# The router of a mixture-of-experts block as four f32r passes with its weights stationary, its results moved by 32x32 transposes on VectorE and small transfers

## What is computed

```python
x = x + attn(layernorm(x))         # linear attention: Q, K, V by 64; energy = K^T V per sequence
x = x + ffn(layernorm(x))
# ffn, on h = layernorm(x):
scores = sigmoid(h @ Wr)                       # 8 experts
_, idx = top_k(scores + router_bias, 2)
w = take_along_axis(scores, idx); w = w / (sum(w) + 1e-9)
cw = zeros(T, 8).at[rows, idx].add(w)
hid = silu(h @ Wg[e]) * (h @ Wu[e])            # experts 0 to 3, 128 wide
routed = sum_e cw[:, e] * (hid @ Wd[e])
routed += cw[:, 4] * h + cw[:, 6] * h + cw[:, 7] * relu(h)
out = routed + causal_depthwise_conv(h, 4 taps)
```

## Time and profile before

| | us |
|---|---|
| median of 3 executions | 893.69 (892.45 to 894.4) |
| the execution profiled | 893.6 |
| its span in the profile | 891.8 |
| PE busy | 855.9 |
| DVE busy | 741.1 |
| ACT busy | 628.7 |
| POOL busy | 572.7 |

### The profile page before, as it was taken

One profiled execution on the slowest core, in us unless ns is written; L12 is line 12 of the kernel. 1 busy time (PEld: TensorE's weight loads), 2 busy tenths in 40 slices (PEclk: granted clock), 3 DMA queues, 4 the chain that ended last, 5 costly groups with the idle time before them and its releaser, 6 DMA issues.

```text
span 891.8 us, 16729 instructions
## 1 busy us (share of the span) xinstructions
PE 855.9 (96%) x5437; PEld 754.3 (85%) x5437; DVE 741.1 (83%) x2056; ACT 628.7 (71%) x1238; POOL 572.7 (64%) x654
## 2 busy tenths in 40 slices
PE   5789999999999999999999999999999999999997
PEld 4668989898888888988889888888888898788876
DVE  5758889988888998888898888899888887767775
ACT  5676777777687777778677777777777775655643
POOL 3336776667676657667666767666576766556663
PEclk9989999999999999999999999999999999999999
DMA  9111434543334543343544343454424344433333
GB/s 286 57 52 47 137 121 142 143 117 99 95 119 142 144 142 68 114 129 120 143 143 114 101 115 99 143 144 142 119 72 119 101 114 119 111 104 100 106 91 84
DMA packets 79446, 103.86 MB, mean 116 GB/s; under 512 B 6528, under 2 KB 58880, under 8 KB 79360
## 3 DMA queue, kind: packets, MB, share of 16 engines
q1 hardware_dynamic: 74752, 86.02, 30.4%
q0 software_dynamic: 4608, 16.78, 10.0%
HBM read 68.96 MB, written 17.04 MB: 96 GB/s over the span
## 4 chain that ended last, share of the span: by engine, by line
PE 66%; DVE 13%; POOL 12%; issue 5%; ACT 4%; DMA 0%; POOLq 0%; ACTq 0%; DVEq 0%
PE ps_gu L406 9%; PE ps_gu L408 9%; PE ps_gu L407 9%; POOL enx L1368 7%; PE ps_y L406 5%; PE ps_y L408 5%; PE ps_y L407 5%; PE ps_sh L543 4%; PE ps_sh L533 3%; POOL gate L1327 3%; PE ps_sh L516 2%; DVE stats L1065 2%; DVE acc L1057 2%; ACT x L840 2%; PE ps_y L456 2%
## 5 line engine op out<-in xcount | busy, mean ns | idle before, releaser
L1327 POOL TENSOR_TENSOR gate<-gate,cwb 128x512 f32<-128x512 f32 x128 | 167.5, 1309 | 127.8 <-ACT gate L763 126.4
L406 PE MATMUL ps_gu<-x2T_hi,wgu_hi 128*128 128x512 f32 x512 | 212.2, 414 | 0.0
L408 PE MATMUL ps_gu<-x2T_hi,wgu_lo 128*128 128x512 f32 x512 | 203.0, 396 | 0.0
L407 PE MATMUL ps_gu<-x2T_lo,wgu_hi 128*128 128x512 f32 x512 | 202.2, 395 | 0.0
L1368 POOL TENSOR_TENSOR enx<-inv_e,logits 128x32 f32<-128x32 f32 x32 | 177.5, 5546 | 8.6 <-ACT logits L756 8.6
L406 PE MATMUL ps_y<-wd_hi,hid_hi 128*128 128x256 f32 x512 | 152.8, 299 | 4.0 <-DVE hid_lo L1018 3.1
L1029 DVE SCALAR_TENSOR_TENSOR conv<-x2T,conv_w,conv 128x512 f32<-128x512 f32 x192 | 146.4, 801 | 0.0
L408 PE MATMUL ps_y<-wd_hi,hid_lo 128*128 128x256 f32 x512 | 145.3, 284 | 0.0
L407 PE MATMUL ps_y<-wd_lo,hid_hi 128*128 128x256 f32 x512 | 144.2, 282 | 0.0
L1011 DVE TENSOR_TENSOR hid<-ps_gu,gate 128x512 f32<-128x512 f32 x128 | 86.0, 672 | 39.2 <-POOL gate L1327 38.1
L408 PEld LDWEIGHTS ps_gu<-x2T_hi,wgu_lo 128*128 128x128 f32 x512 | 96.9, 189 | 22.5
(11 more groups left out here) (115 smaller groups left out, 1934.3 us busy)
## 6 DMA issues: line engine op xcount, KB each, us to landing
cwb<-cw_rows SPq DMA_DIRECT2D x128, 256.0 KB, 4.0
xa<-in_x SPq DMA_DIRECT2D x32, 512.0 KB, 7.5
acc<-in_x SPq DMA_DIRECT2D x32, 512.0 KB, 6.7
acc<-x POOLq DMA_DIRECT2D x32, 512.0 KB, 4.6
out<-acc SPq DMA_DIRECT2D x64, 256.0 KB, 2.3
cwb<-in_wg SPq DMA_DIRECT2D x4, 128.0 KB, 4.0
cwb<-in_wu SPq DMA_DIRECT2D x4, 128.0 KB, 3.8
cwb<-in_wd SPq DMA_DIRECT2D x1, 512.0 KB, 4.5
```

Source lines behind the costliest of these rows:

```text
L406: nc.tensor.matmul(dst, a_hi, b_hi, start=start, stop=False, skip_group_check=True)
L407: nc.tensor.matmul(dst, a_hi, b_lo, start=False, stop=False, skip_group_check=True)
L408: return nc.tensor.matmul(dst, a_lo, b_hi, start=False, stop=stop, skip_group_check=True)
L1327: g.tensor_tensor(gate[:, e % 2], gate[:, e % 2], cwb[:, q, e], ALU.mult).then_inc(gatew_ready, 1)
```

## The change

The router's weights are split into a high part and a low rest, side by side in 32 columns (`wr2`: 8 high, 8 low, 16 zeros), and are now the stationary operand; the two f32r parts of `x2T`, which exist already, stream against them in four passes of 512 columns. The result lies in `ps_sh` with the experts on 32 partitions. DVE turns it by 32x32 blocks (`logits_turn`) and adds the high and low columns (`summed`), and SP moves the four blocks of 32 tokens to their partitions by four transfers within SBUF (`move_logits`). ACT forms from the logits |x|, |x| plus a tiny number and silu of minus that (`score_size`, `score_dip`), and DVE makes the sigmoid of it with a reciprocal, a product, a comparison and a maximum at the start of the routing (`route_scores`, `route_weights`). POOL's `power` is gone. The epsilon of the weights' sum stands in a ninth column of `raw`, so that one small addition goes. DVE turns the columns of `cw` by 32x32 blocks to `cwT`, PE's transpose and ACT's copy of them go, and SP stores them by four transfers instead of one. The halo copy goes from DVE to ACT.

The orders of the head and of the rounds are written anew. In the head the transposes of the first five groups use the banks of `ps_y` and `ps_gu` in turn, the gram matrices and the chain come ahead of them, and one attention (not two) ahead of the first router. In the rounds the order on DVE changes, and in the drain that on DVE, ACT and PE.

PE in a plain round, from the third product of the experts to the fourth, before. `L406` to `L408` are the three passes of a product, `L543` is the router.

The diff, cut to its core:

```diff
+            def move_logits(st):
+
+                sp.wait_ge(sum_ready, st.before("R", 1, 1))
+                if st.later("R", 1):
+                    sp.wait_ge(cw_ready, st.before("R"))
+                for j in range(P // SQ):
+                    sp.dma_start(logits[j * SQ:(j + 1) * SQ, :], summed[:, j].rearrange("p t e -> p (t e)"))\
+                        .then_inc(logits_loaded, 16)
...
-                sp.dma_start(rows.rearrange("a e (t n) -> (a e t) n", t=TG), cwT[:, :]).then_inc(cw_stored, 16)
-                sp.wait_ge(cw_stored, st.before("R", 16, 16))
+                for j in range(P // SQ):
+                    sp.dma_start(rows[:, :, :].rearrange("a e (t n) -> (a e t) n", t=TG)[:, j * SQ:(j + 1) * SQ],
+                                 cwT[j * SQ:j * SQ + EM * TG, :]).then_inc(cw_stored, 16)
+                sp.wait_ge(cw_stored, st.before("R", 64, 64))
...
             def router(st):
-                pe.wait_ge(x2T_ready, st.before("R", HC, HC))
+                if st.before("R") == 0:
+                    pe.wait_ge(wrlo_out, 1)
+                b, q = ps_sh[0][0:SQ, :], st.slot("R", 2)
                 pe.wait_ge(x2Tlo_ready, st.before("R", HC, 1))
-                b, q = ps_sh[0], st.slot("R", 2)
-                for t in range(TG):
-                    for c in range(HC):
-                        last = nc.tensor.matmul(b[:, t * NE:(t + 1) * NE],
-                                                x2T[:, q, c, PAD + t * P:PAD + (t + 1) * P], wr_sb[:, c],
-                                                start=(c == 0), stop=(c == HC - 1))
+                pe.wait_ge(x2Thi_ready, st.before("R", HC, HC))
+                for c in range(HC):
+                    nc.tensor.matmul(b, wr2[:, c], x2T_hi[:, q, c], start=(c == 0), stop=False,
+                                     skip_group_check=True)
+                for c in range(HC):
+                    if c == 1:
+                        pe.wait_ge(x2Tlo_ready, st.before("R", HC, HC))
+                    last = nc.tensor.matmul(b, wr2[:, c], x2T_lo[:, q, c], start=False, stop=(c == HC - 1),
+                                            skip_group_check=True)
...
-                if st.before("B") == 0:
-                    pe.wait_ge(xnTlo_ready, 2 * HC - h)
-                elif st.before("B") == 1:
-                    pe.wait_ge(x1_ready, 1 + h)
-                elif h == 0:
+                if st.before("B") == 1:
+                    pe.wait_ge((x2Tlo_ready, turn_ready)[h], (HC, 1)[h])
+                elif st.before("B") > 1 and h == 0:
                     pe.wait_ge(x2Tlo_ready, st.before("R", HC, HC))
-                else:
-                    pe.wait_ge(logits_ready, st.before("R", 1, 1))
...
+            head_bank = [ps_y, ps_gu, ps_y, ps_gu, ps_y]
+
+            def head_transpose(n):
+                if n >= 2:
+                    pe.wait_ge(xnTlo_ready, (n - 1) * HC)
+                elif n == 1:
+                    pe.wait_ge(wqlo_out, 1)
+                pe.wait_ge(xn_ready, (n + 1) * TG)
+                for c in range(HC):
+                    xn_move(at("A", n, NG), c, head_bank[n][c])
+
...
                     q_project(st)
                 if a_on:
                     gram_halves(st)
-                if r_on:
-                    weights_transpose(st)
+                if b_on and drain:
+                    down(st, "C", 2)
                 if a_on and r_on:
                     xn_transpose(st, 0)
-                if c_on:
+                if c_on and not (b_on and drain):
                     down(st, "C", 2)
                 if a_on and r_on:
...
-            def logits_copy(st):
-                act.wait_ge(router_done, st.before("R", 1, 1))
-
+            def halo(st):
+
+                q = st.slot("R", 2)
                 if st.later("R", 1):
-                    act.wait_ge(enx_ready, st.before("R"))
-                copy(logits[:, :], ps_sh[0][:, 0:TG * NE]).then_inc(logits_ready, 1)
+                    act.wait_ge(x2T_ready, st.before("R", HC))
+                if st.later("R", 2):
+                    act.wait_ge(conv_ready, st.before("R", CT, -CT))
+                if st.first("R"):
+                    copy(x2T[:, q, :, 0:PAD], ident[:, 0:HC * PAD].rearrange("p (c n) -> p c n", c=HC), 0.0)\
+                        .then_inc(halo_ready, 1)
+                else:
+                    copy(x2T[:, q, :, 0:PAD], x2T[:, 1 - q, :, GT:GT + PAD]).then_inc(halo_ready, 1)
+
+            def score_size(st):
+                act.wait_ge(logits_loaded, st.before("R", 64, 64))
+                if st.later("R", 1):
+                    act.wait_ge(cw_ready, st.before("R"))
+                nc.scalar.activation(size[:, :], logits[:, :], ACT.Abs).then_inc(size_ready, 1)
+                act.wait_ge(size_ready, st.before("R", 1, 1))
+                nc.scalar.activation(mag[:, :], size[:, :], ACT.Identity, bias=least[:, :]).then_inc(mag_ready, 1)
+
+            def score_dip(st):
+
+                act.wait_ge(mag_ready, st.before("R", 1, 1))
+                nc.scalar.activation(dip[:, :], mag[:, :], ACT.Silu, scale=-1.0).then_inc(dip_ready, 1)
 
             def conv_begin(st):
...
                 if c_on:
                     silu(st, 2)
                     hid_high(st, 1)
-
+                if r_on:
+                    score_size(st)
+                    score_dip(st)
+                if c_on:
                     q = st.slot("C", 2)
...
+                if c_on and st.drain():
+                    hid_high(st, 2)
+                    silu(st, 3)
                 if r_on:
                     conv_begin(st)
-                if c_on:
+                if c_on and not st.drain():
                     silu(st, 3)
                     hid_high(st, 2)
                 if st.on("L"):
                     norm1(st)
...
-                dve.wait_ge(den_ready, st.before("R", 1, 1))
-                done(v.reciprocal(flat(score[:, :, :]), den[:, :]))
+                return issued, after, done
+
+            def route(st):
+                route_scores(st)
+                route_weights(st)
+
+            def route_scores(st):
+                issued, after, done = counted(st, 0)
+
+                dve.wait_ge(mag_ready, st.before("R", 1, 1))
+                done(v.reciprocal(rmag[:, :], mag[:, :]))
+                dve.wait_ge(dip_ready, st.before("R", 1, 1))
+                after()
+                done(v.tensor_tensor(minor[:, :], dip[:, :], rmag[:, :], ALU.mult))
+                after()
+                done(v.scalar_tensor_tensor(signed[:, :], logits[:, :], 0.0, minor[:, :], ALU.is_gt, ALU.add))
+                after()
...
-                done(v.scalar_tensor_tensor(raw[:, :, :], marked[:, :, 0:NE], TAKEN, score[:, :, :],
+                done(v.scalar_tensor_tensor(raw[:, :, 0:NE], marked[:, :, 0:NE], TAKEN, score[:, :, :],
...
-                done(v.tensor_scalar(wsum_eps[:, :], wsum[:, :], EPS_W, None, ALU.add))
-                after()
...
+                dve.wait_ge(cw_ready, st.before("R", 1, 1))
+                if st.later("R", 1):
+                    dve.wait_ge(cw_stored, st.before("R", 64))
+                v.transpose(cwT[:, :], cw[:, q].rearrange("p e t -> p (e t)")).then_inc(cwT_ready, 1)
+
+            def logits_turn(st):
+                dve.wait_ge(router_done, st.before("R", 1, 1))
+                v.transpose(turned[:, :, :, :].rearrange("p j t n -> p t j n"),
+                            ps_sh[0][0:SQ, :].rearrange("p (t j n) -> p t j n", t=TG, j=P // SQ))\
+                    .then_inc(turn_ready, 1)
+                dve.wait_ge(turn_ready, st.before("R", 1, 1))
+                if st.later("R", 1):
+                    dve.wait_ge(logits_loaded, st.before("R", 64))
+                v.tensor_tensor(summed[:, :, :, :].rearrange("p j t e -> p (j t) e"),
+                                turned[:, :, :, 0:NE].rearrange("p j t e -> p (j t) e"),
+                                turned[:, :, :, NE:2 * NE].rearrange("p j t e -> p (j t) e"), ALU.add)\
+                    .then_inc(sum_ready, 1)
...
 
             def body(st):
                 c_on, y_on, r_on, b_on, m_on = st.on("C"), st.on("Y"), st.on("R"), st.on("B"), st.chain()
-                if r_on:
-                    halo(st)
-                if c_on:
+                if c_on:
+                    if not st.later("C", 1):
+                        x2T_low(st, 0)
+                        x2T_low(st, 1)
                     dve.wait_ge(halo_ready, st.before("C", 1, 1))
                     conv_tap(st, 0)
+                    conv_tap(st, 1)
+                if r_on and st.later("C", 1):
+                    x2T_low(st, 0)
+                if c_on:
+                    conv_tap(st, 2, (0,))
+                if y_on:
+                    output(st, 0)
+                if r_on and st.later("C", 1):
+                    x2T_low(st, 1)
+                if y_on:
+                    output(st, 1)
+                if c_on:
```

(44 more changed lines are left out.)

279 lines of the change are left out of this document (136 added, 143 removed).

## The result

The changed kernel takes 948.13 us (946.68 to 950.32), the kernel before 894.05 us (892.45 to 895.89): a ratio of 1.0589, with a 95% interval of 1.0554 to 1.0624. It is slower by 54 us, where 28 us faster was forecast.

The account below looks back on a forecast made before the run. Two loops of 25.4 us, PE's stream and one through ACT, POOL and DVE, bound the kernel. Plain rounds 6, chain rounds 6, head 5.5 and end 11 us, together 28 off 893.6, gave 866 us, range 848 to 887.

Parts of the forecast that it names:

- the trip of the logits: From DVE's sum through four SP transfers to ACT: three issues of 0.33 us, 1.4 landing and 0.05, together 2.45 us.
- What bounds the kernel: Plain rounds: two loops of 25.4 us, PE's stream and one through ACT, POOL and DVE; a PE gain alone worth nothing.
- PE's stream: Router and weight-column transpose on PE: four passes of 0.23 us, 0.97 us a round saved, plain rounds could be 24.4 us.
- the loop of the prediction: Plain round, hidden product through logits, ACT's queue, gate 3 and hid_low 2 to residual and statistics: 25.5 us.
- (b): Rival on the logits' transfers: landing takes 2.0 us, a plain round 26.1 us, the whole 885 us; chance 0.18.
- (c): Rival on the logits' transfers: the trip sets every round; at 3.0 us landing 27.1 us a round, 906 us; chance 0.09.
- The 25.1 us: Forecast for a plain round, between PE's 24.4 and the loop's 25.5 us; 0.3 us off in each of 20, 6 us.
- The bounds of 24.8 to 25.6 us: DVE's need in a plain round: 24.8 us with today's blocks, 25.6 if the taps meet POOL's gates 0 and 1.
- over 26 us at its worst: DVE's round if POOL's gates block each added two-input operation, by the skill's shared-port rule: over 26 us.
- Chain rounds: The 6 rounds with the attention chain: DVE waits for ACT anyway, so PE's 27.6 us, 1.0 us off each.
- I count nothing: Weight columns' stores on SP: four add 1 us, but columns are ready some 4 us earlier; no effect counted.
- Head and end: Start and drain of the kernel: 5.5 us off in the head (3 to 8), 11 us at the end (6 to 14).

Follow-up runs that it names:

- e8: e2 with the four router passes on PE issued twice, the second set overwriting the first with the same numbers: 923.3 us, ratio 1.0283.
- e2: The changed kernel with ACT's score operations moved behind the first four scalings, so that those run while the logits travel: 911.1 us, ratio 1.0156.
- e7: e2 with POOL's gate weightings 0 and 1 done on only 16 of 512 columns: 889.2 us, ratio 0.9951.
- e4: The changed kernel with DVE's order of taps, first-norm statistics and outputs as in the kernel before, the trip kept: 920.4 us, ratio 1.0257.
- e3: The changed kernel with two idle transfers ahead of the four of the logits, ACT and DVE waiting for all six: 1028.1 us, ratio 1.1466.

## Why the prediction was wrong, step by step

Two steps failed above all: the trip of the logits was priced at 2.45 us and took 3.58, with ACT's whole queue behind it; and DVE, bounded at 25.6 us, needs 26.1 where the trip is hidden.

**What bounds the kernel.** Nothing speaks against it: two loops of 25.4 us on each other, and the gain on PE is worth little alone. No run tests this on the kernel before; e8 bounds what the gain is worth in e2.

**PE's stream.** Right: four passes 0.23 us apart when nothing holds them, and 24.5 us of stream without its waits where 24.4 stood.

**The trip.** The term that failed first. 3 x 0.33 + 1.4 + 0.05 = 2.45 us took its price from the earlier trace rows, a store of 16 partitions to DRAM; the transfer of 32 partitions within SBUF is issued in 0.59 us (median of 128), and lands in 1.7. That is 3.58 us. With it the loop of the prediction, 25.5 us, gives 26.6; the trace has 26.8. It was the mechanism of rivals (b) and (c) with an issue cost that neither had: I had varied the landing alone, and the issue counts three times.

**The 25.1 us.** A round can't be shorter than the longest of its loops. The prediction had one of 25.5 us through ACT, or of 24.7 if hid_low 2 escapes gate 3, and 25.1 is neither. In the changed kernel hid_low 2 does not escape (1.44 us). By that sum a plain round would have gained nothing, even with the trip as priced, so the 6 us for the 20 plain rounds had no ground.

**DVE.** The bounds of 24.8 to 25.6 us were too low; with the trip hidden (e2) it is 26.1. The added operations were sized well: transpose 0.70 (0.65), sum 0.28 (0.3), the three for the score 0.19 to 0.20 each (0.23), `cwT` 0.21 (0.23). Groups of the changed kernel by line: count, busy us, mean ns.

```profile
L1061 DVE SCALAR_TENSOR_TENSOR conv<-x2T,conv_w,conv 128x512 f32<-128x512 f32 x192 | 173.7, 945 | 0.0
...
L1050 DVE TENSOR_TENSOR hid_lo<-hid,hid_hi 128x512 fp32r<-128x512 f32 x96 | 82.6, 860 | 45.3 <-ACT hid_hi L764 45.0
...
L1155 DVE SCALAR_TENSOR_TENSOR raw<-marked,score 128x32 f32<-128x32 f32 x32 | 11.0, 344 | 1.1
```

The blocks by POOL are there. The six taps of a round take 945 ns on average; an unblocked one starts 0.66 us before the next. In the new order both gates 0 and 1 meet taps (1.31 us at 399.27), POOL's hid_lo holds the first of the four that follow it, and hid_low 2 meets gate 3 (1.44 us). `raw` escapes (344 ns on average), but in e2, where the queue is earlier, it is blocked again (median 1.02 us). These blocks were in the upper bound, and well sized: I had counted 0.8 us for gates 0 and 1, e7 shows 0.9; and 22.88 + 1.47 + 0.8 = 25.15 us is what DVE is busy in e2 (25.14). What failed are the waits. The sum took both waits of the kernel before off (2.10 us) and left 0.4 us idle; in e2 0.96 us are left, of them 0.34 ahead of the third hidden product and 0.10 ahead of `minor`. The rule of the Trainium skill (SBUF — State Buffer, the single rule on the shared port pair), from which I had worked out "over 26 us at its worst" through blocks of the added operations, is not how the round got there. The trace agrees with it for the taps, hid_low 2 and `raw`, but the sum (0.28 us) and the operations of the score (0.19) are blocked nowhere in the middle. That 26.1 us is near its estimate is chance.

**Chain rounds.** "DVE waits for ACT anyway, so I take PE's 27.6": wrong, 29.3, and 28.3 with the trip hidden.

**The loads of `cwb`.** Of the columns that are ready some 4 us earlier the prediction said "I count nothing". The stores start 2.9 us earlier (13.9 us after the first router pass, 16.8 before), and the loads behind them now stand beside POOL's accumulating transfer. In a plain round that costs nothing yet (5.6 us to landing instead of 4.6, and norm2 is released by POOL), but where gate 3 is another 1 us late the landing takes 7.4 us and more.

**The clock.** Not in the prediction at all. Two rounds of the middle are 4.3 and 4.6 us longer than the other chain rounds, each with a late landing of the logits, an accumulating transfer of 8.6 us, a long wait of PE (2.60 and 2.26 us) and the lower clock behind it, which is 1.7 us of PE's work in each. Outside the head the clock falls in five places, two in the kernel before.

**Head and end.** 5.5 us and 11 us off were forecast, 3.8 and 14.5 us more came. In the head the transposes went as planned, but DVE's weight split stood ahead of the rows that PE wanted. In the drain two rows tell it, first POOL and DVE in the round of group 27, then POOL in that of group 28:

```profile
814.15 4.11 POOL L1383 TENSOR_TENSOR rstd<-mv,half_neg 128x4 f32<-128x4 f32 x1
```

```profile
814.65 2.72 DVE L1061 SCALAR_TENSOR_TENSOR conv<-x2T,conv_w,conv 128x512 f32<-128x512 f32 x4
```

```profile
837.98 0.93 POOL L1414 DMA_DIRECT2D acc<-x  x1 [5.67 <-ACT x L998]
```

A power of 128x4 takes 4.11 us instead of 1.0, because four taps now stand in a row beside it; norm2 and PE wait 3.8 and 3.5 us for it. In the old order of e4, with two taps beside it, it takes 2.79:

```profile
788.37 2.79 POOL L1381 TENSOR_TENSOR rstd<-mv,half_neg 128x4 f32<-128x4 f32 x1
```

In the drain POOL also issues its accumulating transfer ahead of the factors of norm2; that transfer waits 5.67 us for ACT's second scalings, which the trip holds up. In the prediction I followed POOL's gates behind ACT's queue, but not this transfer, here or in the rounds.

**The rivals.** (c) had the right sign and place and got a chance of 0.09; its price, 906 us at 27.1 us a round, kept the gains of head and end. Since the trip was the longest new path and I knew its parts only from other transfers, (b) and (c) together deserved as much as the forecast.

Sum against the 53 us of span: e2, in which the trip is hidden, gives 35.6 back. The remaining 17.5 are 3.6 at the first router, 0.3 to group 2, 11.5 to group 25 (DVE's 26.1 us), 3.5 in the drain, less 1.6 behind it.

## What to carry to other kernels

A transfer between two engines that work in order is priced as the number of issues times the issue time of its own shape, plus the landing; and where the engine at its end waits, look first for work that may stand ahead of that wait: one move of three instructions was worth 37 us here. When two limits lie on each other, count what a change adds to the third: DVE went from 22.9 to 25.1 us in a round of 25.4, and what was taken off it came back nearly whole (0.88 of 0.90 us in e7). When a part gets ready earlier, ask which transfers it starts and beside what they then run. And take the smallest part of a large change by itself: two of its edits (the columns and one move in the drain) together were the only ones shown to win.

## What the runs showed of the hardware

- SP takes 0.59 us to issue a transfer of 32 partitions x 128 bytes within SBUF (507 ns at least), against 0.33 us for the store of the earlier trace rows; the store of `cwT` in four parts takes 1.73 us, 0.43 each.
- A small POOL operation is held back by DVE's as DVE's is by POOL's: the power of 128x4 waited through four taps that followed each other without a gap (4.11 us instead of 1.0), and through two (2.79 us).
- A wait of PE of 2.60 us was followed by some 3.4 us at the lower clock level, so by another 1.7 us of PE's work. In e3 waits of 2.0 us were followed by it in some rounds and not in others (groups 5 and 9).
- An accumulating transfer of 512 KB issued by POOL lands in 4.5 to 5.6 us when SP's four loads of 256 KB start 4.8 us or more behind its issue, and in 7.4 to 9.2 when they start within 0.4 us of it. With the clock, this is why stretching the trip by 1.2 us a round cost 2.6 (e3).
